# Layer norms: GpSimd gets the mean itself from a doubled (mean, variance) pair; the negated mean on VectorE goes

## The reference

```python
def _layernorm(x, axis=-1, eps=1e-05):
    m = jnp.mean(x, axis=axis, keepdims=True)
    v = jnp.var(x, axis=axis, keepdims=True)
    return (x - m) / jnp.sqrt(v + eps)
...
h = _layernorm(x, axis=-1) * (1 + ca) + sa
x = x + ga * _L0_attn_ref(h, L0_attn_W_qkv, L0_attn_W_out)
h = _layernorm(x, axis=-1) * (1 + cb) + sb
x = x + gb * _L0_ffn_ref(h, L0_ffn_router_w, L0_ffn_wg, L0_ffn_wu, L0_ffn_wd)
```

## Time and profile before

| | us |
|---|---|
| median of 3 runs | 687.18 (686.79 to 688.35) |
| the profiled execution | 687.55 |
| its span | 685.5 |
| TensorE busy in the span | 574.0 (84%) |
| VectorE | 473.4 (69%) |
| ScalarE | 320.7 (47%) |
| GpSimd | 282.6 (41%) |
| nm (L724), 64 times | 9.7, 0.151 each |
| sh1 (L449), 12 times / sh2 (L466), 32 times | 2.6, 0.220 each / 6.1, 0.191 each |

### The profile page before, as it was taken

The page is one execution under the profiler, slowest core; times in us unless marked ns, Lnnn a source line. Parts: engine busy times, 40 slices in busy tenths (PEclk is TensorE's granted clock), DMA queues, the critical chain, the costliest instruction groups (busy, mean ns, idle before and its releaser), DMA issues.

```text
span 685.5 us, 13772 instructions
## 1 busy us (share of the span) xinstructions
PE 574.0 (84%) x4041; PEld 535.6 (78%) x4041; DVE 473.4 (69%) x1304; ACT 320.7 (47%) x717; POOL 282.6 (41%) x427
## 2 busy tenths in 40 slices
PE   2999878999899400239999999999999999999990
PEld 2677667888777300139999999999999999999990
DVE  2578989998677777777747756767577566666431
ACT  4577757887444310014435535444355444454430
POOL 5689857887578400030305207034061070341304
PEclk9999999999899655559999999999999999999995
DMA  4412248744556640043335518326365083250203
GB/s 123 124 54 77 62 133 252 225 130 134 155 181 192 205 111 0 0 133 113 95 93 166 102 35 204 98 64 145 92 177 108 15 209 93 89 121 9 32 1 38
DMA packets 91911, 75.24 MB, mean 110 GB/s; under 512 B 12108, under 2 KB 88278, under 8 KB 91864
## 3 DMA queue, kind: packets, MB, share of 16 engines
q1 hardware_dynamic: 82872, 58.77, 28.7%
q0 software_dynamic: 8992, 15.90, 11.3%
HBM read 52.48 MB, written 22.16 MB: 109 GB/s over the span
## 4 chain that ended last, share of the span: by engine, by line
PE 56%; DVE 19%; issue 6%; POOL 2%; DMA 1%; DVEq 1%; ACT 1%; SPq 0%; POOLq 0%; ACTq 0%
PE bank L1319 33%; PE bank L1331 16%; DVE feat L823 2%; PE bank L1282 2%; DVE hit L876 2%; DVE x L842 2%; DVE st L844 1%; PE bank L1296 1%; PE bank L1237 1%; DVE den_r L829 1%; DVE mv L719 1%; POOL out L505 1%; DVE rot_b L805 1%; DVE rot_b L807 1%; DMA xg<-h_rows,g_idx 1%
## 5 line engine op out<-in xcount | busy, mean ns | idle before, releaser
L1319 PE MATMUL bank<-xT_h,w_h 128*128 128x320 f32 x512 | 159.6, 312 | 1.7 <-DVE xT_l L1022 1.7
L1319 PE MATMUL bank<-xT_l,w_h 128*128 128x320 f32 x512 | 159.0, 311 | 0.0
L1319 PE MATMUL bank<-xT_h,w_l 128*128 128x320 f32 x512 | 158.9, 310 | 0.0
L495 POOL DMA_INDIRECT xg<-h_rows,g_idx x40 | 43.8, 1095 | 271.3 <-DVE g_idx L995 261.6
L1050 DVE TENSOR_TENSOR hid<-act_g,bank 128x320 f32<-128x320 f32 x128 | 62.2, 486 | 70.5 <-ACT act_g L647 70.5
L647 ACT ACTIVATE act_g<-bank 128x320 f32<-128x320 f32 x128 | 56.0, 437 | 102.8 <-PE bank L1319 102.4
L651 ACT CAST hid_h<-hid 128x320 fp32r<-128x320 f32 x128 | 58.9, 460 | 93.7 <-DVE hid L1050 93.7
L1319 PEld LDWEIGHTS bank<-xT_h,w_h 128*128 128x128 f32 x512 | 97.5, 190 | 2.1 <-DVE w_l L1009 2.1
L1319 PEld LDWEIGHTS bank<-xT_h,w_l 128*128 128x128 f32 x512 | 97.3, 190 | 0.0
L1319 PEld LDWEIGHTS bank<-xT_l,w_h 128*128 128x128 f32 x512 | 97.3, 190 | 0.0
L1331 PE MATMUL bank<-w_h,hid_h 128*128 128x256 f32 x320 | 91.5, 286 | 0.4 <-DVE hid_l L1055 0.4
(11 more groups left out here) (180 smaller groups left out, 1154.3 us busy)
## 6 DMA issues: line engine op xcount, KB each, us to landing
w_raw<-wg SPq DMA_DIRECT2D x32, 256.0 KB, 3.3
w_raw<-wu SPq DMA_DIRECT2D x32, 256.0 KB, 4.3
w_raw<-wd SPq DMA_DIRECT2D x16, 512.0 KB, 5.5
x_in<-x SPq DMA_DIRECT2D x32, 128.0 KB, 2.1
q_store<-qT SPq DMA_DIRECT2D x32, 128.0 KB, 1.8
q_in<-q_store SPq DMA_DIRECT2D x32, 128.0 KB, 2.2
x_re<-x SPq DMA_DIRECT2D x32, 128.0 KB, 2.2
out<-x SPq DMA_DIRECT2D x32, 128.0 KB, 1.9
```

Source lines behind the costliest of these rows:

```text
L495: nc.gpsimd.indirect_dma_start(out=xg[par][:, a, :], out_offset=None, in_=h2_rows, in_offset=bass.IndirectOffsetOnAxis(ap=g_idx[par][:, a: ...
L1319: last = MM(bank[2 * h + m][:, 0:HCAP], W[i][:, f, at:at + P], XT[j][:, k, cols], start=n == 0, stop=n == 3 * KC - 1)
```

## The change

`finish_stats` no longer makes nm. mv gets two buffers, and GpSimd reads the mean out of it: hn becomes (x - mean) * rs, and sh becomes (mean * rs) * -1 as a TENSOR_SCALAR, whose first scalar is the column rs. The waits ahead of sh become waits apart. Since mv is now what GpSimd reads, VectorE's waits for `scale1` and `scale2` stand ahead of `bn_aggr`, no longer ahead of `finish_stats`.

```diff
@@ -211,8 +211,8 @@
         wout_g = [sa(f"wout_g{b}", [P, KC, D]) for b in range(B)]
 
         x_in = [sa(f"x_in{i}", [P, D]) for i in range(2)]
-        st1, mv1 = sa("st1", [P, 6]), sa("mv1", [P, 2])
-        nm1, ve1 = ([sa(f"{n}_{i}", [P, 1]) for i in range(2)] for n in ("nm1", "ve1"))
+        st1, mv1 = sa("st1", [P, 6]), [sa(f"mv1_{i}", [P, 2]) for i in range(2)]
+        ve1 = [sa(f"ve1_{i}", [P, 1]) for i in range(2)]
         rs1, sh1 = sa("rs1", [P, 1]), sa("sh1", [P, 1])
         hn = sa("hn", [P, D])
         hT = sa("hT", [P, KC, P])
@@ -230,8 +230,8 @@
         att, attT = sa("att", [P, D]), sa("attT", [P, D])
         x_re = [sa(f"x_re{i}", [P, D]) for i in range(2)]
         x2 = [sa(f"x2_{i}", [P, D]) for i in range(2)]
-        st2, mv2 = sa("st2", [P, 6]), sa("mv2", [P, 2])
-        nm2, ve2 = ([sa(f"{n}_{i}", [P, 1]) for i in range(2)] for n in ("nm2", "ve2"))
+        st2, mv2 = sa("st2", [P, 6]), [sa(f"mv2_{i}", [P, 2]) for i in range(2)]
+        ve2 = [sa(f"ve2_{i}", [P, 1]) for i in range(2)]
         rs2, sh2 = sa("rs2", [P, 1]), sa("sh2", [P, 1])
         xn2, xm2 = [sa(f"xn2_{i}", [P, D]) for i in range(2)], sa("xm2", [P, D])
         h2 = [sa(f"h2_{i}", [P, D]) for i in range(2)]
@@ -445,13 +445,13 @@
                     wait(pool, norm1, s.t(2))
                     nc.gpsimd.tensor_tensor(rs1[:, :], ve1[s.par(2)][:, :], half_neg[:, :], ALU.pow).then_inc(pow1, 1)
                     if on["att"]:
-                        pool.wait_ge(pow1, s.t(3))
-                        nc.gpsimd.tensor_tensor(sh1[:, :], nm1[s.par(2)][:, :], rs1[:, :], ALU.mult).then_inc(scale1, 1)
+                        wait_apart(pool, pow1, s.t(3), apart)
+                        nc.gpsimd.tensor_scalar(sh1[:, :], mv1[s.par(2)][:, 0:1], rs1[:, :], -1.0, ALU.mult, ALU.mult).then_inc(scale1, 1)
                     else:
                         wait(pool, tr_h, s.t(2))
                         wait_apart(pool, pow1, s.t(3), apart)
-                        nc.gpsimd.tensor_scalar(hn[:, :], x_in[s.par(2)][:, :], nm1[s.par(2)][:, :], rs1[:, :],
-                                                ALU.add, ALU.mult).then_inc(norm1, 1)
+                        nc.gpsimd.tensor_scalar(hn[:, :], x_in[s.par(2)][:, :], mv1[s.par(2)][:, 0:1], rs1[:, :],
+                                                ALU.subtract, ALU.mult).then_inc(norm1, 1)
                         pool.sem_inc(scale1, 1)
                 if on["trh"] and spared(s):
                     wait(pool, hTh_d, s.t(2))
@@ -462,8 +462,8 @@
                     wait(pool, stat2, s.t(o + 1))
                     wait(pool, norm2, s.t(o))
                     nc.gpsimd.tensor_tensor(rs2[:, :], ve2[s.par(o)][:, :], half_neg[:, :], ALU.pow).then_inc(pow2, 1)
-                    pool.wait_ge(pow2, s.t(o + 1))
-                    nc.gpsimd.tensor_tensor(sh2[:, :], nm2[s.par(o)][:, :], rs2[:, :], ALU.mult).then_inc(scale2, 1)
+                    wait_apart(pool, pow2, s.t(o + 1), apart)
+                    nc.gpsimd.tensor_scalar(sh2[:, :], mv2[s.par(o)][:, 0:1], rs2[:, :], -1.0, ALU.mult, ALU.mult).then_inc(scale2, 1)
                 if on["second"]:
                     o = -LAG - 3
                     b = (s.rep + o) // TB
@@ -718,17 +718,16 @@
                 wait_apart(dve, bn, count, apart)
                 V.bn_aggr(mv[:, :], st[:, :]).then_inc(ag, 1)
 
-            def finish_stats(mv, nm, ve, ag, done, count):
+            def finish_stats(mv, ve, ag, done, count):
 
                 dve.wait_ge(ag, count)
-                V.tensor_scalar(nm[:, :], mv[:, 0:1], -1.0, None, ALU.mult)
                 V.tensor_scalar(ve[:, :], mv[:, 1:2], LN_EPS, None, ALU.add).then_inc(done, 1)
 
             def variance2(s, o):
 
-                variance(st2, mv2, bn2, ag2, s.t(o + 1))
                 wait(dve, scale2, s.t(o - 1))
-                finish_stats(mv2, nm2[s.par(o)], ve2[s.par(o)], ag2, stat2, s.t(o + 1))
+                variance(st2, mv2[s.par(o)], bn2, ag2, s.t(o + 1))
+                finish_stats(mv2[s.par(o)], ve2[s.par(o)], ag2, stat2, s.t(o + 1))
 
             def between(s):
 
@@ -808,14 +807,14 @@
                                     cs[:, HALF:2 * HALF].unsqueeze(1).to_broadcast([P, g // 2, HALF]), ALU.mult)\
                         .then_inc(rope_m, 1)
                 if on["stats"]:
-                    variance(st1, mv1, bn1, ag1, s.t(4))
+                    wait(dve, scale1, s.t(2))
+                    variance(st1, mv1[s.par(3)], bn1, ag1, s.t(4))
                 if on["trh"] and not spared(s):
                     wait(dve, hTh_d, s.t(2))
                     V.tensor_tensor(hT_l[s.par(1)][:, :, :], hT[:, :, :], hT_h[s.par(1)][:, :, :].bitcast(F32),
                                     ALU.subtract).then_inc(hTl_d, 1)
                 if on["stats"]:
-                    wait(dve, scale1, s.t(2))
-                    finish_stats(mv1, nm1[s.par(3)], ve1[s.par(3)], ag1, stat1, s.t(4))
+                    finish_stats(mv1[s.par(3)], ve1[s.par(3)], ag1, stat1, s.t(4))
                 if on["feat"]:
                     wait(dve, exp_d, s.t(0))
                     wait(dve, tr_q, s.t(-1))
```

## The result

| | before | after |
|---|---|---|
| median of 4 runs, us | 687.76 (686.79 to 689.36) | 696.30 (694.13 to 698.33) |
| profiled execution, us | 687.55, span 685.5 | 697.11, span 695.2 |
| from the fifth to the fifteenth tile's rot_a (first batch) | 36.51 | 42.75 |
| from there to the 32nd rot_a | 90.92 | 91.76 |
| from there to the last rs | 61.44 | 58.84 |

The ratio of the runs is 1.0105, with a 95% interval of [1.0084, 1.0126]: 5.8 to 8.7 us slower. I had forecast 686.1. `rot_a` is one of VectorE's instructions, once per tile, and serves as milepost. The two profiled executions lie 9.7 us of span apart.

The account below looks back on a forecast made before the run. GpSimd fills the first batch (0); a feat/rot collision loop sets two-batch steps; VectorE, then GpSimd's chain, the tail. -1.18 - 0.07 + 0.14 - 0.44 + 0.42 = -1.13 gives 686.4 profiled, 686.1 median; range 684.3 to 689.2.

Parts of the forecast that it names:

- The step that failed: First batch, 20 to 90 us, GpSimd's hn: only an operand's name and add against subtract differ, so 0.
- the stretch 20 to 90 us changed at all: Sign that the forecast is wrong: any change in the first batch, one norm per tile, which was put at 0.
- The dear sh: Rival, chance 0.10: a one-column TENSOR_SCALAR sh costs what hn costs, 0.56; +6.9 us in all, 694.1.
- sh and its wait: GpSimd's sh1 and sh2: +0.12 for the wait, +0.09 for TENSOR_SCALAR at 0.28; +0.21 each, bounds -0.10 and +0.37 on the latter.
- nm and the moved wait: VectorE: dropping nm gains 0.07 per instance where VectorE bounds; the scale wait ahead of bn_aggr costs 0.
- The collision: 110.9 to 170 us: rot starting under a running feat makes feat end 0.59 after rot's start and costs rot 0.46; period 5.34.
- Four short steps at -0.54: 110.9 to 170 us: four of eleven steps lose the collision, -0.54 each, seven pay +0.14; together -1.18.
- The tail: Entry +0.14; loop, 193 to 217 us, from 5.44 to 5.33 per two tiles, -0.44; straight part +0.42.
- the straight tail: From 217 us on, chain over GpSimd: three passes of sh2 at 0.21 - 0.07 each, +0.42.

Follow-up runs that it names:

- e1: Changed kernel with hn's subtract as add (wrong value, same shapes and waits): 688.89 us against 689.21 for the kernel before, ratio 0.9998.
- e4: Kernel before with sh1 and sh2 alone changed, to TENSOR_SCALAR with a wait of their own, nm kept: 690.81 us against 689.21, ratio 1.0025.
- e9: GpSimd TENSOR_SCALAR forms put in twice each at 256, 32 and 1 columns, where VectorE has hardly any two-input work; only durations read, rounds agree to 0.02 us.
- e10: Kernel before with ve ahead of nm, both kept, each with its own semaphore: 689.72 us against 689.53, ratio 1.0004.
- e6: Kernel before with an unread GpSimd memset of 0.20 us between h and rot: 691.46 us against 691.61, ratio 0.9994.
- e3: Changed kernel with sh as plain TENSOR_TENSOR without its own wait (wrong sign), hn as before, nm away 44 of 64 times: 685.84 us against 689.21, ratio 0.9958.
- e2: Kernel before with hn alone made subtract, nm holding +mean for the first 20 tiles: 695.54 us against 689.21, ratio 1.0093.
- e5: Kernel before with fourteen GpSimd instructions, mostly TENSOR_SCALAR forms, once each from 232 us on; at 128 columns add, mult 447 ns, subtract, mult 1049.
- e7: Kernel before with nm and ve made by one two-column VectorE instruction, eps added to the mean: 690.33 us against 691.61, ratio 0.9975.

## Why the prediction was wrong, step by step

**The step that failed** is "Its normalisation hn is already a TENSOR_SCALAR there, with the wait of its own. Only the name of an operand and add against subtract differ. I put this stretch at 0." I knew that GpSimd had no idle time there, so that any price for hn would count in full. I gave the new operation the duration of the old one's row because the instruction has the same name. No row of the trace showed a subtract in a TENSOR_SCALAR on GpSimd, so it needed bounds from both sides as sh did, and it got none. The price is 0.67 per hn: +6.2 us in the stretch of the first batch, a ratio of 1.0105 over all runs, while everything that I worked out at length moved nothing that can be measured (e1). The forecast did name "the stretch 20 to 90 us changed at all" as a sign that it was wrong.

**The dear sh** (694.1) came nearest in time, but as a mechanism it is refuted: sh takes 0.26. The dear one was the instruction that this rival used as its measure.

**sh and its wait.** Forecast 0.28 and +0.12; measured 0.264 and +0.13 (e4: ten steps +1.95, so 0.20 each). Right. The way to 0.28 was partly luck: I had argued that "most of hn must be its 256 columns", and e9 gives these 0.22 of 0.55. From the Trainium skill, page "GPSIMD Engine Reference", section "Elementwise — side-by-side cycle accounting", I had estimated 0.22 for hn's columns and 0.34 for the fixed part, and e9 agrees with that estimate (0.22, and 0.33 at one column with two column scalars); sh is cheaper since one of its scalars is an immediate (0.25). The same section doesn't set pairs of operations apart, and here measurement decides: 0.85 ns a column with `add, mult`, 3.5 with `subtract, mult`.

**nm and the moved wait.** I had 0.07 for nm and 0 for the wait. mv to ve was 0.34 (115.87 to 116.21) and is 0.20 (123.28 to 123.48). 0.07 is nm; the other 0.07 goes with the wait for scale that no longer stands between mv and its reader. e10 keeps the wait there and puts ve first, and mv to ve is 0.27. Before, and in e10:

```profile
115.87 0.17 DVE L719 BATCH_NORM_AGGREGATE mv<-st 128x2 f32<-128x6 f32 x1
```

```profile
116.87 0.16 DVE L722 BATCH_NORM_AGGREGATE mv<-st 128x2 f32<-128x6 f32 x1
117.14 0.15 DVE L727 TENSOR_SCALAR ve<-mv 128x1 f32<-128x1 f32 x1
```

**The collision.** The number 0.59 was right and the mechanism wrong, so that its fit was luck. e6 shows that feat's end hangs on h's end, and rot always starts 0.03 to 0.05 before that end, so both readings fit the rows of before. The loop is then: ve to h's end 2.58, feat's end +0.56, next ve +2.20, 5.34. With the new sh the first is 2.81 (123.48 to 126.29), the third 2.07, so 5.43, as measured; e4, with 2.80 and 2.20, gives 5.55 for 5.56 measured. I had 5.48 for such a step. The Trainium skill, page "SBUF — State Buffer", section "Who interferes with whom", calls the ports that the two engines share an exclusive lock. The forecast took from that section that both instructions get slower by their overlap, and set this against my constant. That was a misreading: with a lock only the later one waits, and e6 agrees with that. The 0.55 is what feat still needs after h's end, with 0.69 for a feat alone.

**Four short steps at -0.54.** Two of eleven came, and they brought nothing:

```profile
148.06 1.28 POOL L478 TENSOR_TENSOR h<-xm,mod_all 128x256 f32<-128x256 f32 x1 [0.25 <-POOL xm L474]
149.30 1.29 POOL L483 TENSOR_TENSOR rot<-rot_a,rot_b 128x512 f32<-128x512 f32 x1
```

```profile
148.07 0.67 DVE L822 SCALAR_TENSOR_TENSOR feat<-rot,ex 128x512 f32<-128x512 f32 x1
```

The recorded starts lie 0.01 apart, and here feat was the undisturbed one, so h was held (1.28 for some 0.73) in place of rot. GpSimd's own turn is no shorter, and the step of 5.10 is followed by one of 6.30. I had let rot lose its 0.46 without asking who would wait for feat then. e1, with the same second half, shows the same two short feats and the same pair of steps, 5.10 and 6.31.

**The tail.** In the loop two tiles took 5.44 and take 5.47; I had 5.33.

```profile
206.39 0.42 DVE L841 TENSOR_TENSOR x<-bank,x_re 128x256 f32<-128x256 f32 x1 [0.48 <-PE bank L1236]
...
211.86 0.42 DVE L841 TENSOR_TENSOR x<-bank,x_re 128x256 f32<-128x256 f32 x1 [0.47 <-PE bank L1236]
```

Every second x waited for y before the change too, 0.23 in the earlier trace rows; that wait is now 0.47. So y's turn had no slack of 0.31. e3 and e4 price this loop: without nm and with the plain sh two tiles take 5.28 (-0.16), with the dear sh 5.63 (+0.19), together the 5.47. The 0.20 of a dearer sh counts once in two tiles, and a part of VectorE's gain turns into waiting for y (0.35 in e3). In the straight tail four tiles took 10.09 and take 10.59 (221.57 to 232.16), where I had +0.28 for two of the three passes. Of the +0.50 the first three tiles make 0.14 (7.63 to 7.77, and 7.77 in e1 too). The rest is the last one, whose x waits for a store, since its buffer is still being written out; in e1, with the same code there, it doesn't, and four tiles take 10.24.

```profile
230.68 0.42 DVE L841 TENSOR_TENSOR x<-bank,x_re 128x256 f32<-128x256 f32 x1 [1.42 <-DMA out<-x]
```

**What stays open.** From the 32nd rot_a to the last rs the traces give 61.44 before, 61.07 in e6, 58.84 after, 58.58 in e10; from the last rs to the end 458.2 before, 463.0 after, 464.7 in e6, whose median equals that of before. e2 has the same instructions as the kernel before there, and its two stretches take 60.13 and 461.8. So they differ between single profiled executions by 1.3 and 3.6 us without any change in them. The wait of the last x for a store is one part (1.74 in e6, 1.99 in e3, none before); the rest, most of it behind the attention half, wasn't tried. No part of the verdict rests on them: the ratios of e1 and e2 do. Why GpSimd takes longer for one pair of operations than for another isn't shown either.

## What to carry to other kernels

An operation code is part of an instruction's price: if a change swaps add for subtract, or the order of two operations, look for a row with that very pair, and where there is none give it bounds before anything else, first on the engine that has no idle time. Here `add, mult` with a negated scalar was the cheap pair, and the negation on VectorE that looked superfluous bought it. When two engines hold each other up, ask who came first: the end of the one in progress sets the other's end, a delay of an instruction that is held anyway is free, and a gain often only changes who is held.

## What the runs showed of the hardware

- GpSimd, TENSOR_SCALAR in fp32 with two scalar operands: 0.55 us for 128x256 with `add, mult`, 1.24 with `subtract, mult`; 0.85 against 3.5 ns a column. At 32 columns `mult, add` and `mult, mult` 0.36; `mult, subtract`, `add, add`, `subtract, subtract` 0.46 to 0.48; one operation alone, subtract too, 0.35 to 0.36 (e9). At 128 columns, less clean, one operation alone took 0.60 and `add, mult` 0.45 (e5).
- At one column it costs 0.33, with an immediate as second scalar 0.25; the TENSOR_TENSOR of one column 0.19.
- A feat (VectorE, two SBUF inputs, 0.69 us alone) that starts 0.03 us or more into GpSimd's h, hT_l or rot ends 0.54 to 0.56 us after that instruction does, and even an instruction of two columns is held (0.68 for 0.16, e7). A GpSimd instruction behind it is held in turn (rot 1.73 for 1.27), and where feat gets in first, h is (1.28 for 0.73).
- A further semaphore wait between two dependent instructions of a queue cost 0.07 us on VectorE and 0.06 to 0.10 on GpSimd (e10), though it was met already.
